# A block's high and low half earlier in ScalarE's and VectorE's slots, the silu later, the last recurrences in tiles 11 and 12

## What is computed

```python
x = L0_attn_x
xn = _layernorm(x, axis=-1)
x = x + _L0_attn_ref(xn, ...) + _L0_ffn_ref(xn, ...)

# _L0_attn_ref: gated recurrence in chunks of 64, then a gated FFN
a = sigmoid(h @ w_a + decay_bias); i_gate = sigmoid(h @ w_i); v = h @ w_v
input_signal = sqrt(clip(1 - a * a, 1e-08)) * (i_gate * v)
x = x + _chunked_scan(a, input_signal) @ out_proj_w
gate, up = split(rmsnorm(x) @ w_gate_up, 2)
return x + silu(gate) * up @ w_down

# _L0_ffn_ref: 8 experts, each token goes to its top two
h = square(relu(x_flat @ w_fc[e])); y = h @ w_proj[e]; out = sum(y * w_tok)
```

## Time and profile before

| | us |
|---|---|
| median of 3 runs | 303.07 (302.66 to 304.24) |
| the profiled execution | 304.53 |
| its span | 302.8 |
| TensorE busy | 266.6 (88%) |
| VectorE busy | 213.2 (70%) |
| ScalarE busy | 159.4 (53%) |
| GpSimd busy | 112.4 (37%) |

### The profile page before, as it was taken

The page is one execution under the profiler, slowest core; times in us unless marked ns, Lnnn a source line. Parts: engine busy times, 40 slices in busy tenths (PEclk is TensorE's granted clock), DMA queues, the critical chain, the costliest instruction groups (busy, mean ns, idle before and its releaser), DMA issues.

```text
span 302.8 us, 5115 instructions
## 1 busy us (share of the span) xinstructions
PE 266.6 (88%) x1593; PEld 229.4 (76%) x1593; DVE 213.2 (70%) x402; ACT 159.4 (53%) x323; POOL 112.4 (37%) x136
## 2 busy tenths in 40 slices
PE   5999999999999969968885889789869789899795
PEld 5767788888888858956774778668758679787695
...
GB/s 215 363 383 281 270 113 149 163 281 193 43 81 70 86 76 81 143 151 152 139 141 122 153 135 115 73 211 196 140 108 164 207 104 107 177 68 274 385 174 69
DMA packets 106933, 49.62 MB, mean 164 GB/s; under 512 B 71862, under 2 KB 103612, under 8 KB 106908
## 3 DMA queue, kind: packets, MB, share of 16 engines
...
HBM read 27.32 MB, written 21.96 MB: 163 GB/s over the span
## 4 chain that ended last, share of the span: by engine, by line
PE 50%; DVE 23%; issue 10%; ACT 6%; DMA 6%; SPq 3%; POOL 2%; ACTq 0%; DVEq 0%; POOLq 0%
PE ps L458 42%; PE ps L546 4%; DVE aT_lo L1383 4%; DMA sums<-y_dram 3%; ACT xgT_hi L930 2%; DVE act_e L1367 2%; SPq L401 2%; DVE xgT_raw L1351 2%; DVE gu L1284 2%; DVE cum L1176 2%; DVE xgT_lo L1358 2%; DMA act_dram<-act_e 2%; DVE aT_raw L1376 1%; ACT act_e L941 1%; PE ps L475 1%
## 5 line engine op out<-in xcount | busy, mean ns | idle before, releaser
L1645 POOL DMA_INDIRECT y_dram<-yb,home_u x39 | 38.4, 984 | 94.5 <-ACT yb L960 93.0
L902 ACT ACTIVATE gu<-ps 128x512 f32<-128x512 f32 x31 | 18.5, 597 | 58.5 <-PE ps L458 56.5
L1624 POOL DMA_INDIRECT xs_dram<-rows_x,slot_u x32 | 41.5, 1297 | 11.3 <-issue 10.2
L458 PE MATMUL ps<-h2T_lo,Wgu_hi 128*128 128x512 f32 (+1 forms) x132 | 42.6, 392 | 0.0
L458 PE MATMUL ps<-h2T_hi,Wgu_hi 128*128 128x512 f32 (+1 forms) x132 | 41.8, 398 | 0.0
L458 PE MATMUL ps<-h2T_hi,Wgu_lo 128*128 128x512 f32 (+1 forms) x132 | 40.5, 388 | 0.0
L458 PE MATMUL ps<-Wpj_hi,aT_hi 128*128 x78 | 18.3, 315 | 23.4 <-DVE aT_lo L1383 23.4
L458 PE MATMUL ps<-Wd_hi,guT_hi 128*128 128x256 f32 x128 | 36.9, 288 | 2.3 <-DVE guT_lo L1289 2.2
L1284 DVE TENSOR_TENSOR gu<-gu,ps 128x512 f32<-128x512 f32 x31 | 21.1, 680 | 24.3 <-PE ps L458 24.1
L458 PE MATMUL ps<-Wd_hi,guT_lo 128*128 128x256 f32 x128 | 36.6, 286 | 0.0
L458 PE MATMUL ps<-Wd_lo,guT_hi 128*128 128x256 f32 x128 | 36.5, 285 | 0.0
(11 more groups left out here) (174 smaller groups left out, 605.7 us busy)
## 6 DMA issues: line engine op xcount, KB each, us to landing
...
```

The costliest lines, as they stand in the source:

```text
L458: return nc.tensor.matmul(dst, lhs, rhs, start=start, stop=stop, skip_group_check=group)
L902: A.activation(gu[d % 2][:, :], ps[:, gu_bank(d), :], ACT.Silu).then_inc(sg_ready, 1)
L1624: pool.indirect_dma_start(out=xs_dram, in_=rows_x[:, b, j, :], in_offset=None, out_offset=bass.IndirectOffsetOnAxis(ap=slot_u[:, n:n + 1], ...
L1645: pool.indirect_dma_start(out=y_dram, in_=yb[i % YB][:, :], in_offset=None, out_offset=bass.IndirectOffsetOnAxis(ap=home_u[:, i:i + 1], ax ...
```

## The change

On ScalarE `block_middle` now comes ahead of `block_relu`, and `gate` last in a first slot. On VectorE `block_middle` comes right behind `act_turn` (and `split_gu`), ahead of `up`, `block_turn`, `block_square` and `block_in`. The drain has its silu one block later. Batch 3's recurrence moves to tiles 11 and 12, with two waits of ScalarE for it; `homes` moves from slot 6 to slot 7, and the load of `of_slot` behind the next `load_pair`. The adds of the sums begin in tile 28, not 27. POOL forms the root of batch 1 after two more scatters. No operation is added or taken away.

```diff
-        ADD_SUM = 27
+        ADD_SUM = {28: ((0, 0), (1, 0)), 29: ((0, 1), (1, 1)), 30: ((0, 2), (1, 2), (0, 3))}
...
-                if n == 2:
+                if n == 3:
                     sp.dma_start(of_slot[:, :, :], xs_slot[:, :, WEIGHT:ROW]).then_inc(of_slot_loaded, 16)
...
             def squares(b):
+                if b == 2:
+                    act.wait_ge(rec_ready, K * 3 + 1)
...
                 act.wait_ge(rn2_ready, b + 1)
+                if b == 2:
+                    act.wait_ge(rec_ready, K * B)
...
                             split_gu(d - 1)
-                            gate(d)
+                        block_middle(i - LAG + 1)
                         if i % 2 == 0:
                             block_relu(i // 2 - 1)
-                        block_middle(i - LAG + 1)
-                        if i % 2 == 1:
+                        else:
                             block_in(i // 2 + 1)
+                        if v == 0:
+                            gate(d)
...
-                    gate(d)
                     block_y(d1 - 1)
                     block_middle(d1 + 1)
+                    gate(d)
...
                 if b >= 2:
-                    dve.wait_ge(h2T_done, K * b)
+                    dve.wait_ge(h2T_done, K * 2)
...
                             split_gu(d - 1)
+                        block_middle(i - LAG + 1)
                         if v == 0 and d > FIRST and d % M == 1:
                             take_down(d // M - 1, 1)
                         if v == 1:
                             up(d)
                         if i % 2 == 0:
                             block_turn(i // 2 + 1)
+                            block_square(i // 2 - 1)
                         else:
                             block_in(i // 2 + 1)
-                        if i % 2 == 0:
-                            block_square(i // 2 - 1)
-                        block_middle(i - LAG + 1)
-                        if i == 6:
+                        if i == 7:
                             homes()
-                        if d in (14, 15) and v == 0:
-                            cumulate(3, d - 14)
-                        if (d, v) in ((14, 2), (15, 1)):
-                            recur(3, d - 14)
+                        if d == FIRST:
+                            (cumulate, recur)[v](3, 0)
+                        if d == FIRST + 1 and v < 2:
+                            (cumulate, recur)[v](3, 1)
...
+            store_rows(0, 3, range(0, 2))
             root_h2(1)
-            store_rows(0, 3)
+            store_rows(0, 3, range(2, 4))
```

25 lines of the change are left out of this document (12 added, 13 removed).

## The result

The changed kernel takes 280.28 us (278.66 to 280.65, 4 runs) beside 302.87 us for the kernel before on the same chip: a ratio of 0.9235, with an interval of 0.919 to 0.928. A second set of runs, further down, gave 0.922 (0.918 to 0.926). The forecast was 276, with 270.5 to 287 as its range. The time lies 0.3 us above the forecast's own band (272 to 280, chance 0.57) and at the lower edge of the first rival's (SP or the DMA engines become the bound, 280 to 290, chance 0.25). The profiled execution took 280.65 us, its span is 278.9.

What follows compares the result with a forecast made beforehand. From 131 to 251 us a chain from engine to engine was taken as the bound. Terms -26.0 - 2.0 - 1.7 + 2.0 = -27.7 took the profiled 304.53 to 276.8, 275.4 on the median; forecast 276, range 270.5 to 287.

Steps and rivals of the forecast that it cites:

- first rival: Stage: SP or the DMA engines become the bound as pairs need issues faster; 280 to 290 us, chance 0.25.
- the allowance for SP: Stage: SP's issue sets and its DMAs cost between 0 and +4 us, taken as +2.0.
- level boundaries: Last slots in tiles beginning with an odd slot: low half ready just when TensorE wants it; 0.2 each for five, 1.0.
- the wait behind squares(3): Tile 18: four squares behind the later silu stand ahead of a high half; 0.9 us taken.
- Point 1: Stage, slots 9 to 38: high half first on ScalarE, low half first on VectorE; 89.4 against 115.4 us, -26.0.
- point 2: Slots 1 to 8: last recurrences in tiles 11 and 12 cost +1.1, waits in slots 8 and 9 go, -3.1; -2.0.
- 0 for the drain: Drain: paced by SP, begins with the turn of slot 38 and moves with it; 0 (-0.7 to +2).
- Tail: Tail: adds of sums one tile later remove the first add's wait; last guT_lo sooner, -1.7 us.
- T: Tail: end of tile 28's gate and up matmuls, 279.6 in the kernel before; last guT_lo forecast 16.9 us later.
- Root and of_slot: Root between scatters: 0, at most +0.7 us; of_slot one pair later on SP: 0.
- the wait moves: Stage: a costly level place and one more wait at every tile keep 13 us; 289 us, chance 0.12.
- slower: Stage: crowded DMA engines stretch the aq round trip, holding TensorE at every pair; 307 us at 8.5 a pair, chance 0.03.

Runs made afterwards that it cites:

- e6: Changed kernel with the 512 KB load that adds x to batch 3 issued behind the last scatter, not in tile 22; 275.9 us, ratio 0.908.
- e1: Kernel before with only the new order on ScalarE and VectorE, silu in the drain included; recurrences and sums as before; 285.8 us, ratio 0.940.
- e4: Changed kernel with batch 3's recurrences back in tiles 14 and 15, without the two waits for them; 285.6 us, ratio 0.942.
- e12: Changed kernel with batch 3's 512 KB load behind the last scatter and two tiny extra SP issues per pair; 282.5 us, ratio 0.926.

## Why the prediction held, and where it did not

The time is inside the range, 4.3 us above the forecast, and where the forecast's band and the first rival's meet. The order of events on the three engines is as forecast; the miss is SP's part, and to about 1 us a fall of the clock in the head. From the same sum for the profiled executions, forecast and what each of the two traces of the changed kernel (first, again) shows against the kernel before:

| term | forecast | first | again |
|---|---|---|---|
| slot 0's start | 0 | +0.2 | +1.5 |
| slot 0 to 9 | -2.0 | -0.8 | -1.0 |
| slot 9 to 38, with the allowance for SP | -24.0 | -22.8 | -25.4 |
| slot 38 to 46 | 0 | +1.7 | +3.5 |
| slot 46 to the end | -1.7 | -2.2 | -2.1 |
| sum | -27.7 | -23.9 | -23.5 |

1. *Stage, right.* 89.4 us was worked out for slots 9 to 38 without the allowance. Where SP keeps up (e6) it is 89.17. The places were not all as thought: the level boundaries cost nothing where 1.0 was taken for them, the wait behind squares(3) 0.33 with its restart where 0.9 was taken, and the ten first slots take 36.4 us and not 35.0 (3.50 to 3.90 each), which was in no term.
2. *What it was put down to.* Point 1 gave the whole 26.0 to the order, and point 2 priced the recurrences only where they came, not where they left. By e1 and e4, 7 us of the stage's gain come with the recurrences' leave from tiles 14 and 15, 1.6 of them as a slow stretch. Had they stayed, the sum for the order would have failed: e1 takes 97.3 us from slot 9 to 38 and not 89.4. The sum held only because both parts were in the change; that the two were priced as one is not tested by the total.
3. *Head, right where the clock is.* Undisturbed it is 25.96 to 23.9 or 24.0, -2.0 as forecast; block_in(3) waits 0.55 us and a restart, as forecast (0.7), and the projection starts 0.28 later behind slot 0, as forecast for up(11) (0.3). The waits of slots 8 and 9 went. But a fall of the clock behind the wait at slot 0, seen in most traces, takes 1.1 us of it. No row of the kernel before showed it; in that execution the same wait had no fall.
4. *SP and drain, the term that was mis-sized.* "Between 0 and +4, nearer to the busy stretch: +2.0", and 0 for the drain. Against e6 the two together cost the changed kernel 5.2 us (first: 3.5 from slot 9 to 38, 1.7 behind) and 4.4 (again: 0.9 and 3.5), where 2.0 was allowed. The first rival's mechanism is there, without its steady form: SP isn't the bound through the stage but has half a microsecond a pair to spare, and what it owes is paid at the stage's end. The term was worked out from the length of SP's sets alone. Missing in it is the landing of the stores: ahead of its loads at 218.24 and 229.98 the changed kernel's SP stands 0.7 and 3.5 us until a store has landed, where e6's stands 0 and 1.9 ahead of the same loads. The drain was said to start with the turn of slot 38 and to move with it. It starts from what SP has left undone, and the store it waits for holds the last relu, with the next high half behind it. That relu had no wait of the kind in the kernel before.
5. *Tail, right by its own rows, for the wrong reason.* up_half(0) came 14.7 us after T (257.69) and the last guT_lo 16.8, as worked out. But T + 18.6 in the kernel before held a fall of the clock; without it the old placing ends some 0.6 later, not 1.7.
6. *Root and of_slot.* The root came 0.4 us later and the scatters ended 4.8 sooner, with nothing gained at slot 0, as said: the last weights and the first block on VectorE set that.

The rival "the wait moves" did not come true (no tile of the full order waits at each of its slots), nor did "slower" (e12 with more work on SP is still 7% under the kernel before).
